# Layer norms of a decoder layer: mean and variance merged on VectorE, power and one pass per batch on GpSimd, and a new order of all engines

## The chip, the cores and the metric

The kernel runs on one core of a Trainium2 chip. A core has five engines that matter here: TensorE (PE in the profile; PEld is its weight load), VectorE (DVE), ScalarE (ACT), GpSimd (POOL) and SyncE (SP), whose queue issues all DMAs of this kernel. The metric is the device time of one execution in microseconds; the times given for a kernel are the median of several executions.

## The reference

One decoder layer without an outer batch loop: 64 sequences of 128 tokens with 128 features, a context of 77 tokens for each, 16 heads of 8.

```python
def _layernorm(x, axis=-1, eps=1e-05):
    m = jnp.mean(x, axis=axis, keepdims=True)
    v = jnp.var(x, axis=axis, keepdims=True)
    return (x - m) / jnp.sqrt(v + eps)

x = x + _L0_attn_ref(_layernorm(x, axis=-1), Wq, Wk, Wv, Wo)          # causal, window of 64
x = x + _L0_xattn_ref(_layernorm(x, axis=-1), ctx, ctx, mask, ...)    # 77 context tokens, additive mask
x = x + _L0_ffn_ref(_layernorm(x, axis=-1), W_r, W_k, W_v, mu_r, mu_k)
# ffn: r = sigmoid(xr @ W_r); k = square(relu(xk @ W_k)); out = r * (k @ W_v)
```

Each of the three blocks begins with a layer norm over the 128 features of a token. These norms are what the change is about.

## The kernel before, in words

**Tiles.** The 64 sequences are taken in 16 quads of four (`QB = 4`). A tile of activations is 128 partitions (tokens) by 4 sequences by 128 features, so 128x512. A quad `q` passes through self-attention, cross-attention and the feed-forward part; attention works on pairs `p` of sequences. `score_max` holds scores for the maxima, `score_exp` the scores for the exponentials, and there is one of each in PSUM, so scores, maxima and exponentials alternate on TensorE, VectorE and ScalarE. Two PSUM tiles `proj[0]` and `proj[1]` take all projections and transposes in turn.

**Order.** Every engine has its own list of calls, written out by hand in three parts: `fill()`, `step(s)` for s from 7 to 14, and `drain()`. A step works on several quads at once: it begins quad s, attends to quad s-1, starts the cross-attention's projections of quad s-2, does the cross-attention of s-3 and s-4, and ends the feed-forward part of quads s-4 and s-5. One step takes about 40 us. Each engine runs its list strictly in order; semaphores, with `wait_ge` ahead of an instruction, tie the lists together. A wait holds all that stands behind it on its engine.

**The norms.** There are three per quad, 48 in all: n = 0 on the input `x_in` for the self-attention, n = 1 on `x1` for the cross-attention, n = 2 on `x2` for the feed-forward part. Each goes this way:

1. VectorE, `stats_of` (L1420 to L1428): four `bn_stats`, one per sequence, from 128x128 each to six numbers, which are count, mean and sum of squared deviations of the even columns and of the odd ones.
2. GpSimd, `moments_of` (L643 to L663): three small operations on 128x4 combine both halves (L648 to L650), then three more (L653 to L655), then one (L658) gives four times the variance plus four epsilon; `pow` with -0.5 gives half of the reciprocal root (L660), and one addition doubles it (L663). Each group waits for the one before.
3. GpSimd, `norm_of` (L665 to L674): one pass over 128x512 subtracts the mean (L669), a second multiplies by the reciprocal root (L672), both with a broadcast operand. The output is `xn[n]`.
4. TensorE turns `xn` (`turn_x`, `turn_xc`, `turn_xe`, all with the line of the helper, L2021), ScalarE copies it out of PSUM (`take_xnT`, `take_xcT`, `take_xeT`), and the projections follow.

VectorE's `stats_of` waits before it writes: `ln_moments[n] >= 7 * q` says that GpSimd has used the statistics of the quad before.

**Other work that the text below names.** VectorE: `max_self` (L1553, L1556) and `max_cross` (L1565, `cneg_max`) take the maxima of scores, `copy_low` (L1544, `k_low`) copies key rows in pairs of instructions, `rest_k`, `rest_q`, `rest_ck`, `rest_cq` (L1499, L1501) split projections into bfloat16 parts, `mid_max` and `mid_cross_max` (L1574, L1581, `cmax_mid`) do so for maxima, `spread_v` (L1525, `v_heads`) writes the values, `add_x1` and `add_x2` (L1608, L1617) add the residual, `mix_tokens` (L1626) mixes neighbouring tokens, `split_mask` (L1449 and on, `mask_f`) prepares the mask once at the start. GpSimd: `low_part` (L681) makes the last bfloat16 part, `add_bias` (L689), `step_tokens` (L697), `square_key` (L702), `add_y` (L706), and at the start the fills of `make_self_pads` (L616, `v_even`, `v_odd`) and `make_cross_pads`. SP: the stores of the parts to DRAM (`store_k`, `store_q`, `k_scr`, `q_scr`), their loads in another layout (`load_keys`, `load_queries`, and the cross ones), `load_x`, `load_ctx`, `load_shift`, `load_cross_shift`, `store_y`. ScalarE: exponentials (`exp_self` L964, `exp_cross` L976) and copies, `take_v_odd` (L949) among them. TensorE: `attend_rest`, `attend_cross` (products with the probabilities), `mix_key`, `mix_gate`, `mix_value` of the feed-forward part.

## Time and profile before

| | |
|---|---|
| median of 3 executions | 778.36 us (778.01 to 781.46) |
| the profiled execution, its own time | 780.04 us |
| its span in the profile | 778.2 us |
| mean granted clock of TensorE, share of full | 0.898 |
| busy: PE, PEld, DVE, ACT, POOL | 647.1, 487.2, 515.7, 415.5, 379.6 us |
| DMA | 106.79 MB, 54.9% of 16 engines |
| a step in the middle of the run | about 40 us |

The profile is of one execution. The busy time of an engine is the sum of its instructions; register, branch and DMA-issuing instructions are not in it. The span is what the profile covers, and the execution's own time lies 1.8 us over it. "Idle before" in a row is the time in which an engine had nothing running ahead of that instruction, with what released it. The chain that ended last is followed back from the last instruction, at each step to what released it.

### The profile page before, as it was taken

The numbers are of one execution on the slowest core, as the hardware profiler recorded it, in microseconds if no ns is written. First come the engines' busy times: TensorE is split into PE (matmuls) and PEld (weight loads), VectorE is DVE, ScalarE is ACT, GpSimd is POOL, SyncE is SP. The second block draws the span as 40 slices with busy tenths as digits, with TensorE's granted clock in tenths as the row PEclk, the third lists the DMA queues.
The fourth block names the chain that finished last, engine by engine and source line by source line (L and its number), as shares of the span: only waits on it lengthen the run. The fifth ranks groups of instructions, "written<-read, shape, count | busy, mean of one in ns | idle before, by whom it ended". The sixth has DMA issues, their size and how long they took to land.

```text
span 778.2 us, 32657 instructions
## 1 busy us (share of the span) xinstructions
PE 647.1 (83%) x13935; PEld 487.2 (63%) x13935; DVE 515.7 (66%) x906; ACT 415.5 (53%) x634; POOL 379.6 (49%) x681
## 2 busy tenths in 40 slices
PE   2368778988988899999999999899899987997663
PEld 2247566766666676767677767677776765674442
DVE  8773556777666687777777777767677764754431
ACT  1122525665555666666666666566565663754430
POOL 7732323365444646473746464645365641634413
PEclk9555878999899999999999999999899996998875
DMA  2936585585664857475666666756567663333200
GB/s 69 174 121 88 151 163 159 133 176 141 167 161 104 209 126 195 105 222 114 186 150 169 161 176 149 189 134 174 141 164 169 165 155 53 103 93 101 51 15 13
DMA packets 162102, 106.79 MB, mean 137 GB/s; under 512 B 40531, under 2 KB 149414, under 8 KB 161958
## 3 DMA queue, kind: packets, MB, share of 16 engines
q1 hardware_dynamic: 161958, 104.70, 54.9%
q8 instruction: 111, 1.82, 1.1%
q14 instruction: 33, 0.27, 0.1%
HBM read 53.48 MB, written 50.14 MB: 133 GB/s over the span
## 4 chain that ended last, share of the span: by engine, by line
PE 56%; DVE 14%; POOL 11%; issue 9%; ACT 7%; DMA 2%; POOLq 0%; SPq 0%; DVEq 0%; ACTq 0%
PE sums L2253 5%; PE proj L2177 4%; PE proj L2021 4%; PE score_max L2091 4%; PE sums L2141 3%; PE score_exp L2235 3%; PE score_exp L2122 3%; PE sums L2153 2%; PE proj L2262 2%; PE proj L2201 2%; PE score_max L2220 2%; PE proj L2045 2%; PE proj L2081 2%; PE proj L2051 2%; DVE cneg_max L1565 2%
## 5 line engine op out<-in xcount | busy, mean ns | idle before, releaser
L976 ACT ACTIVATE cprobs<-score_exp 77x1024 f32<-77x1024 f32 x128 | 130.1, 1017 | 58.7 <-PE score_exp L2235 57.3
L1565 DVE TENSOR_REDUCE cneg_max<-score_max 128x8 f32<-128x616 f32 x128 | 102.0, 797 | 42.1 <-PE score_max L2220 40.1
L964 ACT ACTIVATE probs<-score_exp 128x1024 f32<-128x1024 f32 x96 | 97.7, 1018 | 56.8 <-PE score_exp L2122 35.8
L1553 DVE TENSOR_REDUCE neg_max<-score_max 128x8 f32<-128x1024 f32 x64 | 78.1, 1220 | 24.8 <-PE score_max L2091 24.4
L2253 PE MATMUL sums<-cprobs,cv_heads 128*32 128x128 f32 x2048 | 83.3, 294 | 3.5 <-ACT cprobs L976 3.2
L648 POOL TENSOR_TENSOR moments<-stats 128x4 f32<-128x4 f32 x48 | 11.6, 241 | 123.8 <-DVE stats L1428 123.7
L2235 PE MATMUL score_exp<-cq_stack,ck_stack 53*128 53x128 bf16 x1024 | 53.9, 227 | 16.6 <-ACT cprobs L976 15.3
L2021 PE MATMUL proj<-ident,xn 128*128 128x128 f32 x192 | 34.8, 311 | 37.2 <-POOL xn L672 35.6
L2253 PEld LDWEIGHTS sums<-cprobs,cv_heads 128*32 128x32 f32 x2048 | 53.5, 115 | 17.6 <-issue 6.8
L681 POOL TENSOR_TENSOR k_parts<-k_rest,k_parts 128x512 bf16<-128x512 f32 x16 | 18.6, 1162 | 90.7 <-ACT k_parts L879 90.7
L2235 PEld LDWEIGHTS score_exp<-cq_stack,ck_stack 53*128 53x128 bf16 x1024 | 31.2, 98 | 39.5 <-ACT cprobs L976 29.4
L672 POOL TENSOR_TENSOR xn<-xn,rstd 128x512 f32<-128x512 f32 x48 | 50.3, 1047 | 6.9
L660 POOL TENSOR_TENSOR root<-var_eps,neg_half 128x4 f32<-128x4 f32 x48 | 50.0, 1041 | 3.8
L2091 PE MATMUL score_max<-k_stack,q_stack 112*64 112x128 bf16 x1024 | 45.2, 236 | 7.6 <-DVE neg_max L1553 4.2
L1544 DVE COPY k_low<-k_stack 48x1024 bf16<-48x1024 bf16 x64 | 48.5, 798 | 3.1 <-DMA k_stack<-k_scr 2.2
L2021 PEld LDWEIGHTS proj<-ident,xn 128*128 128x128 f32 x192 | 23.7, 156 | 42.4 <-issue 40.5
L2122 PEld LDWEIGHTS score_exp<-q_stack,k_stack 114*128 114x128 bf16 x1024 | 40.2, 102 | 14.0 <-issue 9.5
L2220 PEld LDWEIGHTS score_max<-ck_stack,cq_stack 51*128 51x128 bf16 x1024 | 27.1, 99 | 34.9 <-DVE cneg_max L1565 21.0
L2220 PE MATMUL score_max<-ck_stack,cq_stack 51*128 51x77 bf16 x1024 | 41.8, 204 | 8.0 <-DVE cneg_max L1565 7.2
L2141 PE MATMUL sums<-probs,v_heads 128*32 128x64 f32 x2048 | 45.5, 234 | 2.3 <-ACT probs L964 1.7
L1556 DVE TENSOR_REDUCE neg_max<-score_max 128x16 f32<-128x1024 f32 x32 | 39.0, 1218 | 11.5 <-PE score_max L2104 11.4
L2091 PEld LDWEIGHTS score_max<-k_stack,q_stack 112*64 112x64 bf16 x1024 | 34.1, 119 | 18.1 <-DVE neg_max L1553 7.0
(162 smaller groups left out, 1472.9 us busy)
## 6 DMA issues: line engine op xcount, KB each, us to landing
k_stack<-k_scr SPq DMA_DIRECT2D x32, 384.0 KB, 5.0
q_stack<-q_scr SPq DMA_DIRECT2D x32, 384.0 KB, 5.2
cq_stack<-cq_scr SPq DMA_DIRECT2D x64, 192.0 KB, 3.5
ck_stack<-ck_scr SPq DMA_DIRECT2D x64, 125.1 KB
k_scr<-k_parts SPq DMA_DIRECT2D x16, 384.0 KB
q_scr<-q_parts SPq DMA_DIRECT2D x16, 384.0 KB, 3.4
cq_scr<-cq_parts SPq DMA_DIRECT2D x16, 384.0 KB
x_in<-in_x_dram SPq DMA_DIRECT2D x16, 256.0 KB, 4.1
```

Source lines behind the costliest of these rows:

```text
L672: nc.gpsimd.tensor_tensor(xn[n][:, :, :], xn[n][:, :, :], rstd[n][:, :].unsqueeze(2).to_broadcast([P, QB, D]), ALU.mult)\
L964: nc.scalar.activation(probs[:, k, :], score_exp[:, :], ACT.Exp).then_inc(exp_done, 1)
L976: nc.scalar.activation(cprobs[0:TC, n % CSLOTS, :], score_exp[0:TC, :], ACT.Exp).then_inc(cexp_done, 1)
L1553: nc.vector.tensor_reduce(neg_max[p][:, :, k, 1], score_max[:, :].rearrange("p (g k) -> p g k", g=G), AX_X, ALU.max, negate=True).then_inc ...
L1565: nc.vector.tensor_reduce(cneg_max[p][:, :, :, a, b], score_max[:, :].rearrange("p (j c) -> p j c", j=2)[:, :, 0:4 * TC] .rearrange("p j ( ...
L2021: last = nc.tensor.transpose(dst[:, rows * b:rows * b + rows], src[0:rows, b, :], ident[0:rows, 0:rows])
L2091: last = nc.tensor.matmul(score_max[HALF * a:HALF * a + HALF, T * g:T * g + T], q_stack[0:ROW1, p, a, g, b, HALF:T], k_stack[0:ROW1, p, a, ...
L2122: last = nc.tensor.matmul(score_exp[:, c:c + HALF], k_stack[0:ROWS_SELF, p, a, g, b, :], q_stack[0:ROWS_SELF, p, a, g, b, HALF:T], start=T ...
L2141: last = nc.tensor.matmul(sums[0][32 * i:32 * i + 32, b, a, HALF:T], v_heads[:, a, PB * p + b, g, :], probs[:, 2 * b, c:c + HALF], start=( ...
L2220: last = nc.tensor.matmul(score_max[:, c:c + TC], cq_stack[r:r + SHIFT_CROSS, p, i, a, b, :], ck_stack[r:r + SHIFT_CROSS, p, i, a, TC * b: ...
L2235: last = nc.tensor.matmul(score_exp[:, c:c + T], ck_stack[r:r + ROWS_CROSS, p, i, a, TC * b:TC * b + P], cq_stack[r:r + ROWS_CROSS, p, i, ...
L2253: last = nc.tensor.matmul(sums[1][32 * i:32 * i + 32, b, a, :], cv_heads[:, a, PB * p + b, g, :], cprobs[:, n % CSLOTS, c:c + T], start=(j ...
```

## The change

VectorE gets the merging of the statistics: after the four `bn_stats` it does four `bn_aggr`, one per sequence, each from six numbers to mean and variance, and one addition of epsilon to the four variances. Before the first `bn_aggr` it waits for the previous norm's `xn` of the same kind (`ln_out[n]`), since that pass reads `moments[n]`. `moments_of` is gone from GpSimd. `norm_of` waits for the variances, does the `pow`, waits for it, and then does one `tensor_scalar` for each of the four sequences, which subtracts the mean and multiplies by the reciprocal root, both given as one value per partition. The lists of all engines are in a new order: most of `fill()` and `drain()` have swaps of neighbours, and `step()` has a few.

```diff
-        moments = [sb(f"moments{n}", [P, 6, QB]) for n in range(3)]
+        moments = [sb(f"moments{n}", [P, QB, 2]) for n in range(3)]
         var_eps = [sb(f"var_eps{n}", [P, QB]) for n in range(3)]
-        root = [sb(f"root{n}", [P, QB]) for n in range(3)]
...
-        ln_root = [sem(f"ln_root{n}") for n in range(3)]
-        ln_centred = [sem(f"ln_centred{n}") for n in range(3)]
+        ln_var = [sem(f"ln_var{n}") for n in range(3)]
...
-            def moments_of(n, q):
-                pool.wait_ge(ln_stats[n], QB * q + QB)
...
             def norm_of(n, src, q, turned):
                 if later(q):
                     pool.wait_ge(turned, q)
-                mean = moments[n][:, 3, :].unsqueeze(2).to_broadcast([P, QB, D])
-                nc.gpsimd.tensor_tensor(xn[n][:, :, :], src[:, :, :], mean, ALU.subtract).then_inc(ln_centred[n], 1)
+                pool.wait_ge(ln_var[n], q + 1)
+                nc.gpsimd.tensor_tensor(rstd[n][:, :], var_eps[n][:, :], neg_half[:, :], ALU.pow).then_inc(ln_rstd[n], 1)
                 pool.wait_ge(ln_rstd[n], q + 1)
-                pool.wait_ge(ln_centred[n], q + 1)
-                nc.gpsimd.tensor_tensor(xn[n][:, :, :], xn[n][:, :, :],
-                                        rstd[n][:, :].unsqueeze(2).to_broadcast([P, QB, D]), ALU.mult)\
-                    .then_inc(ln_out[n], 1)
+                for b in range(QB):
+                    nc.gpsimd.tensor_scalar(xn[n][:, b, :], src[:, b, :], moments[n][:, b, 0:1], rstd[n][:, b:b + 1],
+                                            ALU.subtract, ALU.mult).then_inc(ln_out[n], 1)
...
                 if later(q):
-                    dve.wait_ge(ln_moments[n], 7 * q)
+                    dve.wait_ge(ln_moments[n], QB * q)
                 for b in range(QB):
                     nc.vector.bn_stats(stats[n][:, b, :], src[:, b, :]).then_inc(ln_stats[n], 1)
+                if later(q):
+                    dve.wait_ge(ln_out[n], QB * q)
+                for b in range(QB):
+                    dve.wait_ge(ln_stats[n], QB * q + b + 1)
+                    nc.vector.bn_aggr(moments[n][:, b, :], stats[n][:, b, :]).then_inc(ln_moments[n], 1)
+                dve.wait_ge(ln_moments[n], QB * q + QB)
+                nc.vector.tensor_scalar(var_eps[n][:, :], moments[n][:, :, 1], EPS, None, ALU.add).then_inc(ln_var[n], 1)
```

Waits of others on `ln_out`, `xn` among them, count four per quad in place of one. The moves in `step()`, engine by engine (SP, GpSimd, ScalarE, VectorE, TensorE):

```diff
-                load_x(q0)
                 load_cross_shift(q4, 1)
+                load_x(q0)
...
-                load_cross_queries(q3, 1)
                 load_cross_keys(q3, 1)
+                load_cross_queries(q3, 1)
...
                 norm_of(0, x_in[q0 % XSLOTS], q0, xnT_made)
-                add_y(q5)
                 low_part(k_parts, 0, k_rest, 1, k_left, k_mid, k_lo, k_stored, 48, q0)
                 low_part(q_parts, 2, q_rest, 1, q_left, q_mid, q_lo, q_stored, 48, q0)
-                moments_of(1, q2)
+                add_y(q5)
                 norm_of(1, x1[q2 % XSLOTS], q2, xcT_made)
...
-                take_v_odd(q1)
                 exp_cross(q4, 1, 1)
                 exp_cross(q4, 1, 2)
                 take_attT(q2, proj[(s + 1) % 2])
                 take_xnT(q0, proj[s % 2])
                 exp_cross(q4, 1, 3)
+                take_v_odd(q1)
...
+                take_cross_sums(q4, 1)
                 mid_q(q0)
-                take_cross_sums(q4, 1)
...
-                mid_max(q1, 1, proj[s % 2])
                 max_cross(q3, 1, 1)
+                mid_max(q1, 1, proj[s % 2])
...
-                attend_cross(q4, 1, 0, 0)
                 pe.wait_ge(v_ready, 3 * q1 + 2)
                 turn_sums(q2, 1, proj[s % 2])
                 pe.wait_ge(cexp_done, 8 * q4 + 6)
                 cross_scores(q4, 1, 1, 0)
+                attend_cross(q4, 1, 0, 0)
...
+                attend_cross(q3, 0, 1, 0)
                 pe.wait_ge(max_mid_ready, 2 * q1 + 2)
                 turn_xe(q4, proj[s % 2])
-                attend_cross(q3, 0, 1, 0)
...
+                pe.wait_ge(exp_done, 6 * q1 + 5)
+                scores_upper(q1, 1, 1)
                 pe.wait_ge(relu_ready, q4 + 1)
                 mix_gate(q4, proj[(s + 1) % 2])
-                pe.wait_ge(exp_done, 6 * q1 + 5)
-                scores_upper(q1, 1, 1)
```

At the start VectorE's list has these moves: `make_low_rows(0)` now stands ahead of the second `stats_of`, `split_mask` behind `order_biases`, and the fills for the second pair and the values of quad 0 change places; TensorE turns quad 1 and projects its keys before the first scores.

## Rows read from the trace of the kernel before

**Rows 1.** Page, first part, busy share of each engine
```profile
PE 647.1 (83%) x13935; PEld 487.2 (63%) x13935; DVE 515.7 (66%) x906; ACT 415.5 (53%) x634; POOL 379.6 (49%) x681
```

**Rows 2.** Page, fourth part, chain that ended last, by engine
```profile
PE 56%; DVE 14%; POOL 11%; issue 9%; ACT 7%; DMA 2%; POOLq 0%; SPq 0%; DVEq 0%; ACTq 0%
```

**Rows 3.** Windows; busy us of PE, PEld, DVE, ACT, POOL (instructions), clock, DMA
```profile
84.00:281.30 197.30, 170.89 (x3916) 128.51 (x3915) 129.42 (x236) 109.14 (x167) 92.55 (x175) 0.91 0.66 158
281.30:568.00 286.70, 263.57 (x6093) 201.64 (x6093) 215.07 (x379) 180.10 (x274) 156.99 (x288) 0.97 0.63 161
363.20:403.30 40.10, 36.90 (x871) 28.18 (x871) 30.87 (x55) 25.79 (x40) 22.47 (x42) 1.00 0.65 164
...
300.00:304.00 4.00, 2.72 (x128) 2.07 (x116) 3.87 (x6) 2.60 (x4) 3.55 (x5) 1.00 0.79 168
...
544.00:548.00 4.00, 2.13 (x96) 1.56 (x85) 3.55 (x5) 0.60 (x1) 2.58 (x4) 0.98 0.83 171
548.00:552.00 4.00, 3.55 (x52) 2.68 (x52) 1.08 (x2) 3.04 (x5) 1.94 (x2) 0.50 0.24 91
```

**Rows 4.** Waits of TensorE, until 300 us and from 300 to 600 us
```profile
PE proj L2021 <- POOL xn L672: 28.1, 7, 12.0
...
PE score_exp L2235 <- ACT cprobs L976: 9.8, 15, 0.9
```

**Rows 5.** Timeline of TensorE, its three longest waits for `xn`
```profile
12.02 1.09 PE L2021 MATMUL proj<-ident,xn 128*128 128x128 f32 x4 [12.02 <-POOL xn L672]
32.91 1.09 PE L2021 MATMUL proj<-ident,xn 128*128 128x128 f32 x4 [10.54 <-POOL xn L672]
...
763.38 1.09 PE L2021 MATMUL proj<-ident,xn 128*128 128x128 f32 x4 [7.06 <-POOL xn L672]
```

**Rows 6.** Timeline of all engines, the norm of `x_in` in a step
```profile
357.64 0.86 DVE L1428 BATCH_NORM_STATS2 stats<-x_in 128x6 f32<-128x128 f32 x4
...
358.58 0.20 POOL L648 TENSOR_TENSOR moments<-stats 128x4 f32<-128x4 f32 x1 [4.64 <-DVE stats L1428]
...
359.94 0.69 DVE L1525 COPY v_heads<-proj 128x512 f32<-128x512 f32 x1 [1.12 <-PE sums L2153]
...
362.64 1.04 POOL L672 TENSOR_TENSOR xn<-xn,rstd 128x512 f32<-128x512 f32 x1
...
363.82 0.63 PE L2021 MATMUL proj<-ident,xn 128*128 128x128 f32 x4
```

**Rows 7.** Groups of GpSimd by line: a pass and the power
```profile
L672 POOL TENSOR_TENSOR xn<-xn,rstd 128x512 f32<-128x512 f32 x48 | 50.3, 1047 | 6.9
L660 POOL TENSOR_TENSOR root<-var_eps,neg_half 128x4 f32<-128x4 f32 x48 | 50.0, 1041 | 3.8
```

**Rows 8.** Groups of VectorE by line and shape
```profile
L1428 DVE BATCH_NORM_STATS2 stats<-x 128x6 f32<-128x128 f32 x128 | 27.8, 279 | 0.6
...
L1478 DVE COPY bias_cols<-sums 128x3 f32<-128x3 f32 x1 | 0.1, 145 | 0.0
...
L1372 DVE MEMSET neg_half<- 128x4 f32 x1 | 0.1, 62 | 0.8 <-PEq L3370 0.8
```

**Rows 9.** Timeline of VectorE, idle time behind the other two norms' statistics
```profile
370.87 0.28 DVE L1581 TENSOR_TENSOR cmax_mid<-proj,cmax_hi 32x128 bf16<-32x128 f32 x1 [0.93 <-ACT cmax_hi L957]
...
381.39 0.75 DVE L1501 SCALAR_TENSOR_TENSOR cq_rest<-proj,bias_cols,cq_parts 128x512 f32<-128x512 f32 x1 [0.82 <-ACT cq_parts L875]
```

**Rows 10.** Timelines of VectorE and GpSimd; line L1544, ns min/median/max
```profile
10.90 4.66 DVE L1449 TENSOR_SCALAR mask_f<-mask_in 16x308 f32<-16x308 int32 x1
...
14.45 0.95 POOL L616 MEMSET v_odd<- 128x1024 f32 x1
...
363.97 1.56 DVE L1544 COPY k_low<-k_stack 48x1024 bf16<-48x1024 bf16 x2
...
383.31 2.02 DVE L1544 COPY k_low<-k_stack 48x1024 bf16<-48x1024 bf16 x2
...
L1544 DVE COPY k_low<-k_stack x64: 418/487/3815, 31.4 to 666.8; 48x1024 bf16<-48x1024 bf16 x64
```

953 lines of the change are left out of this document (457 added, 496 removed).

## The prediction

> **What bounds the kernel now.** The busy shares come first [rows 1]: TensorE leads with 83%, VectorE has 66%, GpSimd 49%. The chain that ended last says the same with one more name in it: 56% TensorE, but also 14% VectorE and 11% GpSimd, some 86 us of 778 [rows 2]. Averages over stages with different limits can mislead, so the windows come next [rows 3]. In the undisturbed step (363.2 to 403.3) TensorE is busy 36.9 of 40.1 us at full clock, VectorE 30.9, GpSimd 22.5. TensorE is the bound there and only 3.2 us a step can be won. Over the seven steps from 281.3 to 568 it is idle 23.1 us (286.7 less 263.6), and a step takes 41.0 us.
>
> The waits of TensorE tell what the norms cost it [rows 4]. Up to 300 us it waits 28.1 us in 7 waits for `xn`, the output of a norm; between 300 and 600 that wait is absent and the largest is 9.8 us for ScalarE's exponentials. Three single waits carry most of the total [rows 5]: 12.02 us at the start, 10.54 us before the second quad's turn, 7.06 us in the tail. What is left of the first 300 us is 28.1 - 12.0 - 10.5 = 5.5 us in five waits.
>
> **The chain of one norm.** In a step [rows 6] the statistics run from 357.64 to 358.50, GpSimd starts at 358.58, `xn` ends at 363.68, and TensorE turns it at 363.82. From statistics to `xn` it is 5.2 us: 2 x 1.04 the two passes over 512 columns, 1.04 the power, and the remaining 2.1 the seven small operations and the doubling, 0.2 us each, with their gaps [rows 6, 7].
>
> **VectorE's part.** It gets four aggregations of six numbers, a wait for the last, and one 4-column addition, 48 times. No such operation is in the trace. From below stands the 62 ns fill of 128x4 [rows 8], from above a statistics instruction, four of them in 0.86 us and 0.28 us for one alone [rows 6, 8]. I take a little less than the 145 ns of the 128x3 copy, the nearest in size [rows 8], as neighbours overlap: 5 x 0.12, and 0.1 us estimated for the wait, about the gap at GpSimd's hand-over [rows 6]. That is 0.7 us a norm; bounds 5 x 0.06 + 0.1 = 0.4 and 5 x 0.28 = 1.4. A step has three norms: 2.1 us, 30.9 to 33.0 of 40.
>
> What hides it: behind the three statistics of a step VectorE sits idle within one or two instructions: 1.12 us before `v_heads` [rows 6], 0.93 before `cmax_mid` and 0.82 before `cq_rest` [rows 9]. Each holds 0.7. I cost the addition at nothing in the step. If the cover is gone, every 0.1 us over it is 0.3 us a step. The third is the tight one: the maximum right behind the statistics of `x2` frees the score bank for the next maxima.
>
> **GpSimd's part.** Seven small operations and the doubling go, and 2 x 1.04 us of passes become four passes of 128 columns. From below a 4-column operation lasts 0.2 us [rows 6]; from above that plus a quarter of 1.04 is 0.46. I take 0.33, in the middle, 1.3 us in all (0.8 to 1.8). The chain is then 0.7 + 0.1 + 1.04 + 0.1 + 1.3 = 3.2 us, 2.0 us shorter (by the bounds 0.7 to 2.8). GpSimd's load falls from 22.5 by 3 x (8 x 0.2 + 2.1 - 1.3) to about 15 us a step.
>
> **A lock between the two engines.** `mask_f`, 16x308, takes 4.66 us and ends at 15.56, just after GpSimd's fill of `v_odd` ends at 15.40; `k_low` has a median of 0.49 us, so a pair takes about 1.0, but in the step one pair takes 1.56, beside `add_y`, and the other 2.02, beside the passes of the `x2` norm [rows 10]. So these copies wait for a running GpSimd instruction. The norm of `x2` will be done about 2 us earlier, before its pair begins, and `add_y` is moved away from the other: up to 0.6 + 1.0 us a step.
> The Trainium skill, "SBUF — State Buffer", section "Who interferes with whom", speaks against the change here: copy, cast and tensor_scalar may take VectorE's two-port mode, and then wait for a whole GpSimd instruction; the new addition of epsilon is a tensor_scalar. The trace agrees for `mask_f`. By that rule the sum would gain up to one GpSimd instruction, 1.04 us, at each norm.
>
> **The sum, by stage.**
> Start: the first norm is on the path, 2.0 us of 12.02. But VectorE's second `stats_of` now waits for the first `xn` before it aggregates, and the ordering of the biases, the mask and `rest_k` queue behind it. Behind that the chain goes through DMAs of `k_scr` and `q_scr`, which only move. The 10.54 us wait shrinks, but the first keys are awaited too. Taken: -2.0 (0 to -3).
> Build-up, 84 to 281: five waits of 5.5 us together, each shorter than the 2.0 us won; what is late next (projections' outputs, exponentials) takes a third back. Taken: -3.5 (0 to -5.5).
> Steps: TensorE is not seen waiting for `xn`; the turn of `xn` follows it by 0.14 us [rows 6], and of the 1.6 us of collisions [rows 10] the second stands ahead of `cneg_max`, for which TensorE waits; part of it pays for the 0.7 us of VectorE ahead. I take 0.5 us a step from both, eight steps: -4.0 (+4 to -9).
> Tail: the last norm is alone on the path, -2.0, and I add an estimated -0.4 for the norms of the two quads before, which wait beside other work: -2.4 (-0.7 to -3.2).
> Moved steps, at 0 each: on SP's queue `load_x` goes behind the two DMAs of a cross shift, whose wait now holds it too, but its tile is read only by the last statistics of the step; the swap of cross keys and queries exchanges like with like, and the stores behind keep their place. On GpSimd's queue `add_y` goes behind the k and q parts, which wait for ScalarE; `add_x2` waits for it, and comes later in the step. TensorE turns `xe` and does `mix_gate` behind one group of products each; the mixing behind it waits for a maximum on VectorE anyway. ScalarE's copy of `v_odd` goes behind three exponentials and is read by `attend_rest`, a third of a step on. If a cover fails, the moved work is late by what it was moved past, at most one exponential (1 us) a step; I allow -1 to +3 us for all of them.
> Sum: -2.0 - 3.5 - 4.0 - 2.4 = -11.9. The profiled execution took 780.04 us (span 778.2); it lies 1.7 above the median 778.36. So 768.1 for such an execution, and 766.5 as the median.
>
> **The rivals.**
> Hidden anyway. TensorE is the bound and no wait for `xn` stands in the steps [rows 3, 4]. Only the tail and 1 us at the start remain: 775.4. Against it: five waits in the build-up.
> More than forecast. A step in the middle takes 41.0 us on average and 40.1 undisturbed, and in 548 to 552 TensorE ran at a granted clock of 0.50, the lower of its two levels (1.2 GHz), right behind 4 us in which it was busy 2.1 [rows 3]. If the shorter chain removes the idle time ahead of such stretches, 0.9 us in each of seven steps come back: 766.5 - 6 = 760.5. For it: a clock mean of 0.97 and 0.91 in two stages. Against: the idle time there is mostly VectorE's and ScalarE's.
> VectorE becomes the bound: slower. Place: the third statistics of a step, ahead of the maximum and the `k_low` copies. It decides when a norm adds more than its gaps hold, 0.96 us on average; at 1.2 the gains are eaten (0.24 x 3 x 13 steps = 9.4, and the gain of the steps with it). At the upper bound of 1.4 it costs 0.44 x 3 x 13 = 17 us: 783.5. For it: VectorE is busy 3.9 of 4 us in 300 to 304, and TensorE only 2.7 [rows 3]. Against: small operations are cheap there.
> The lock at every norm: slower. If the addition of epsilon waits as `mask_f` and `k_low` do [rows 10], its cost hangs on GpSimd. Busy 15 of 40 us with instructions of 1.04 at most, GpSimd is met in four cases of ten and for half an instruction, 0.2 us a norm, which the gaps hold. A whole instruction each time would make 0.7 + 1.04 = 1.74, 0.78 over the gaps, 30 us in all: 796.5.
> The change does not do what it says: four passes at 0.46 us with two scalars each cost 1.8 of the 2.2 they replace. Then a norm wins 1.5 of the 2.0 us, a quarter of the sum goes, and the time is 769.5; it falls in the forecast's own range.
>
> **How the numbers follow.** A measurement of this kernel can tell about 0.5%, 3.9 us: 774.5 and 782.3 are the bounds. Chances: forecast (762 to 774.5) 0.50; more than forecast 0.18; hidden anyway 0.20; slower by VectorE 0.09; by the lock 0.03. Faster 0.68, same 0.20, slower 0.12. The range, 755 to 782, takes in the larger gain, the hidden case, and leaves most of the slow case out.
>
> **What would show it.** Right: aggregations near 0.12 us apart; four passes of 0.3 to 0.35; `xn` about 3.2 us behind the statistics; the tail wait 5 us in place of 7.06; the five early waits gone; `k_low` pairs near 1.0 us; steps of 40 us. Wrong: VectorE busy over 34 us a step, waits of TensorE for `cneg_max` grown, the addition of epsilon at 0.5 us or more (the lock), or a start no earlier because VectorE waits for `xn`. A new idle stretch from the reordering alone would show as a wait for something that no norm feeds.

## The result, and the profile after

The changed kernel takes 802.63 us (median of 4 executions, 795.49 to 805.95). The kernel before, run beside it on the same chip, takes 779.91 us. The ratio is 1.0268, with an interval of 1.0179 to 1.0356: slower by about 21 us, where a gain of 12 was forecast, and outside the range. The profiled execution took 801.91 us with a span of 800.1. The ratios here and below leave out every execution over 1.5% above the fastest of its own kernel, and so they can differ from the quotient of the two medians.

The first and fourth parts of the page:

```profile
PE 642.9 (80%) x13935; PEld 485.1 (61%) x13935; DVE 520.0 (65%) x1146; ACT 418.0 (52%) x634; POOL 364.2 (46%) x393
...
PE 49%; DVE 15%; POOL 14%; issue 9%; ACT 6%; DMA 5%; SPq 1%; POOLq 0%; DVEq 0%; ACTq 0%
```

TensorE's busy time fell by 4 us against [rows 1] while the span grew by 22, so the loss is idle time. The working said that GpSimd falls from 22.5 to about 15 us a step, which over 16 quads is 120 us; in the whole run it fell by 15, from 379.6 to 364.2. On the chain GpSimd went from 11 to 14% and TensorE from 56 to 49% [rows 2].

The groups of GpSimd and VectorE by line and shape (busy us, mean ns of one, idle before):

```profile
L648 POOL TENSOR_SCALAR xn<-x,moments,rstd 128x128 f32<-128x128 f32 x128 | 104.5, 829 | 3.3
...
L648 POOL TENSOR_SCALAR xn<-x_in,moments,rstd 128x128 f32<-128x128 f32 x64 | 53.6, 848 | 1.7
...
L645 POOL TENSOR_TENSOR rstd<-var_eps,neg_half 128x4 f32<-128x4 f32 x48 | 52.1, 1085 | 130.6 <-DVE var_eps L1383 130.5
...
L1499 DVE COPY k_low<-k_stack 48x1024 bf16<-48x1024 bf16 x64 | 28.6, 487 | 3.9 <-DMA k_stack<-k_scr 2.9
...
L1383 DVE TENSOR_SCALAR var_eps<-moments 128x4 f32<-128x4 f32 x48 | 19.9, 416 | 1.6
...
L1381 DVE BATCH_NORM_AGGREGATE moments<-stats 128x2 f32<-128x6 f32 x192 | 17.4, 152 | 2.3 <-POOL xn L648 2.3
```

A pass over 128 columns takes 0.83 us on average, not 0.33: the four of a norm take 3.14 us in the timeline below, more than the two wide passes of 1.04 [rows 7] that they replace. The 192 passes cost 158 us, where the 96 wide ones cost 100. The small operations that went away pay for that and for VectorE's new part, and little more, and so the norm hardly got shorter. This is the norm of `x_in` in a step, the answer to [rows 6], in the timeline of all engines:

```profile
367.78 0.86 DVE L1376 BATCH_NORM_STATS2 stats<-x_in 128x6 f32<-128x128 f32 x4
...
368.57 0.36 DVE L1381 BATCH_NORM_AGGREGATE moments<-stats 128x2 f32<-128x6 f32 x4
...
368.96 0.17 DVE L1383 TENSOR_SCALAR var_eps<-moments 128x4 f32<-128x4 f32 x1
...
369.28 1.03 POOL L645 TENSOR_TENSOR rstd<-var_eps,neg_half 128x4 f32<-128x4 f32 x1 [5.18 <-DVE var_eps L1383]
...
370.41 3.14 POOL L648 TENSOR_SCALAR xn<-x_in,moments,rstd 128x128 f32<-128x128 f32 x4
...
373.98 0.60 PE L1983 MATMUL proj<-ident,xn 128*128 128x128 f32 x4
```

From the end of the statistics (368.64) to the end of `xn` (373.55) it is 4.9 us, against 5.2 before and 3.2 forecast. VectorE's share of it is 0.5 us at this norm, at the low end of its term; one of the other two norms of a step is dearer, as the part on the lock says.

TensorE's waits until 300 us (total, times, longest) answer to [rows 4]:

```profile
PE proj L1983 <- POOL xn L648: 31.3, 8, 11.6
PE score_max L2053 <- DVE neg_max L1508: 6.1, 5, 2.2
PE score_max L2066 <- DVE neg_max L1508: 3.4, 5, 1.3
```

The waits for `xn` did not shrink, they grew from 28.1 to 31.3 us. Where the time went is read best from when VectorE begins the statistics of `x_in` of each quad (a table made from the timelines, us; the third kernel is norms_only of the next section, the last one is the kernel before with a test of single operations behind its whole work):

| quad | 3 | 4 | 5 | 6 | 7 | 14 | 15 | end |
|---|---|---|---|---|---|---|---|---|
| before | 107.2 | 146.6 | 187.2 | 231.4 | 275.7 | 562.3 | 601.1 | 778.2 |
| after | 107.0 | 139.7 | 190.9 | 241.2 | 287.6 | 576.6 | 615.8 | 800.1 |
| changed norms, old order | 107.2 | 144.7 | 189.5 | 229.9 | 275.5 | 557.1 | 600.3 | 777.2 |
| before, in probe | 102.1 | 142.2 | 183.1 | 223.3 | 264.7 | 550.1 | 592.5 | |

After is 7 us ahead of before at quad 4 and 12 behind at quad 7. The seven steps add 2.4 us, the tail 7. Each line is one execution, and such a clock scatters: the last line runs the same instructions up to its tail as the first, and is 11 us ahead of it at quad 7. Five profiles with the changed norms and the old build-up until there begin quad 6 between 226.4 and 231.9 us (norms_only, old_fill, new_step_only, new_step_old_pool, fill_c). So a difference of 4 or 5 us between two such lines says little. The changed kernel's 241.2 at quad 6 is beyond it, and the other two profiles with the whole new build-up and these norms agree, with 239.6 and 241.9. The windows say the same (columns as in [rows 3]); after, then before:

```profile
130.00:180.00 50.00, 41.57 (x1022) 30.72 (x1019) 32.45 (x73) 28.24 (x42) 18.77 (x21) 0.94 0.67 147
180.00:230.00 50.00, 41.04 (x947) 31.06 (x944) 35.36 (x73) 29.10 (x45) 23.20 (x25) 0.97 0.60 140
230.00:290.00 60.00, 50.77 (x1163) 38.79 (x1165) 39.45 (x90) 31.04 (x48) 24.64 (x26) 0.94 0.63 136
```

```profile
130.00:180.00 50.00, 45.05 (x1121) 33.40 (x1118) 36.07 (x62) 31.32 (x47) 22.49 (x41) 0.95 0.69 163
180.00:230.00 50.00, 45.16 (x973) 34.04 (x973) 32.38 (x60) 29.10 (x46) 22.38 (x41) 0.93 0.59 146
230.00:290.00 60.00, 54.10 (x1207) 40.20 (x1205) 42.75 (x82) 35.13 (x56) 31.01 (x56) 0.97 0.62 141
```

TensorE is busy 133.4 of these 160 us, 144.3 before. The mean granted clock is nearly the same in both (0.94, 0.97, 0.94 and 0.95, 0.93, 0.97), so the clock is not what took the time.

### The profile page after: what moved, and what is told of

Read it like the earlier page. It is cut to its first block, busy times and chain, and to the rows that moved or that the text cites. A ratio compares the mean times of both kernels' runs of the same rounds, so it can differ in the third digit from the quotient of the medians.

```text
span 800.1 us, 32606 instructions
## 1 busy us (share of the span) xinstructions
PE 642.9 (80%) x13935; PEld 485.1 (61%) x13935; DVE 520.0 (65%) x1146; ACT 418.0 (52%) x634; POOL 364.2 (46%) x393
## 4 chain that ended last, share of the span: by engine, by line
PE 49%; DVE 15%; POOL 14%; issue 9%; ACT 6%; DMA 5%; SPq 1%; POOLq 0%; DVEq 0%; ACTq 0%
POOL xn L648 8%; PE sums L2215 5%; PE proj L2139 4%; PE score_exp L2197 3%; PE proj L1983 3%; PE sums L2103 3%; PE sums L2115 3%; POOL rstd L645 3%; DMA q_stack<-q_scr 3%; PE proj L2224 3%; PE score_max L2053 3%; PE score_exp L2084 2%; PE score_max L2182 2%; PE proj L2007 2%; PE proj L2163 2%
## 5 line engine op out<-in xcount | busy, mean ns | idle before, releaser
L1520 DVE TENSOR_REDUCE cneg_max<-score_max 128x8 f32<-128x616 f32 x128 | 102.1, 798 | 43.1 <-PE score_max L2182 42.4
L645 POOL TENSOR_TENSOR rstd<-var_eps,neg_half 128x4 f32<-128x4 f32 x48 | 52.1, 1085 | 130.6 <-DVE var_eps L1383 130.5
L648 POOL TENSOR_SCALAR xn<-x,moments,rstd 128x128 f32<-128x128 f32 x128 | 104.5, 829 | 3.3
L1508 DVE TENSOR_REDUCE neg_max<-score_max 128x8 f32<-128x1024 f32 x64 | 78.0, 1218 | 29.0 <-PE score_max L2053 28.6
L648 POOL TENSOR_SCALAR xn<-x_in,moments,rstd 128x128 f32<-128x128 f32 x64 | 53.6, 848 | 1.7
L2084 PE MATMUL score_exp<-q_stack,k_stack 114*128 114x64 bf16 x1024 | 43.5, 198 | 3.0 <-ACT probs L912 2.5
```

Of the source, the lines that this page charges most:

```text
L645: nc.gpsimd.tensor_tensor(rstd[n][:, :], var_eps[n][:, :], neg_half[:, :], ALU.pow).then_inc(ln_rstd[n], 1)
L648: nc.gpsimd.tensor_scalar(xn[n][:, b, :], src[:, b, :], moments[n][:, b, 0:1], rstd[n][:, b:b + 1], ALU.subtract, ALU.mult).then_inc(ln_ou ...
L1508: nc.vector.tensor_reduce(neg_max[p][:, :, k, 1], score_max[:, :].rearrange("p (g k) -> p g k", g=G), AX_X, ALU.max, negate=True).then_inc ...
L1520: nc.vector.tensor_reduce(cneg_max[p][:, :, :, a, b], score_max[:, :].rearrange("p (j c) -> p j c", j=2)[:, :, 0:4 * TC] .rearrange("p j ( ...
L2084: last = nc.tensor.matmul(score_exp[:, c:c + HALF], k_stack[0:ROWS_SELF, p, a, g, b, :], q_stack[0:ROWS_SELF, p, a, g, b, HALF:T], start=T ...
```

## The experiments

Executions of one kernel scatter by 5 to 20 us (eleven of the kernel before on one chip lie between 763.2 and 784.9), and so ratios are given with their intervals, and traces are used to place a loss. "Old order" is the order of the kernel before in `fill()`, `step()` and `drain()`.

**The change cut in two.** norms_only has the changed norms in the old order; the other has the old norms in the new order, with `moments_of` directly ahead of each `norm_of`, where the kernel before has it at all but two places.

```diff
 # norms_only
-                mean = moments[n][:, 3, :].unsqueeze(2).to_broadcast([P, QB, D])
+                for b in range(QB):
+                    nc.gpsimd.tensor_scalar(xn[n][:, b, :], src[:, b, :], moments[n][:, b, 0:1], rstd[n][:, b:b + 1],
...
 # order_only, TensorE and GpSimd
-                turn_att(2, proj[1])
+                turn_x(4, proj[1])
+                pe.wait_ge(att_ready, 6)
+                turn_att(2, proj[0])
...
-                add_y(q5)
...
+                add_y(q5)
+                moments_of(1, q2)
                 norm_of(1, x1[q2 % XSLOTS], q2, xcT_made)
```

> The changed norms (merge on VectorE, power, four narrow passes on GpSimd) in the order of before. Theory A, the narrow passes: each lasts 0.83 us instead of the 0.33 that I took, so the loss of some 22 us is theirs and stays here: 795 to 802 us. Theory B, the new order: a norm takes 4.9 us from its statistics to its output in the changed kernel's step against 5.2 before, so in the old order nothing is lost: 774 to 781 us. Theory C, VectorE's added 0.9 us a norm: loss spread evenly over the steps, 785 to 795 us.

Measured: 781.88 us, ratio 1.0080 (1.0024 to 1.0135). That is 0.9 us above the range of theory B and far below those of A and C.

> The norms of before in the new order, each moments_of right ahead of its norm_of. Theory A: the order is harmless, 775 to 782 us. Theory B: the loss is here, 795 us or more, most of it between 140 and 290 us and in the tail.

Measured: 810.91 us, ratio 1.0384 (1.0292 to 1.0475). Theory B holds. The norms alone cost a little instead of gaining; the larger part is the order.

**The narrow passes taken back**: VectorE still merges, GpSimd has two wide passes again. Once in the old order, once in the changed kernel.

```diff
-                for b in range(QB):
-                    nc.gpsimd.tensor_scalar(xn[n][:, b, :], src[:, b, :], moments[n][:, b, 0:1], rstd[n][:, b:b + 1],
-                                            ALU.subtract, ALU.mult).then_inc(ln_out[n], 1)
+                nc.gpsimd.tensor_tensor(xn[n][:, :, :], src[:, :, :], moments[n][:, :, 0:1].to_broadcast([P, QB, D]),
+                                        ALU.subtract).then_inc(ln_centred[n], 1)
+                pool.wait_ge(ln_centred[n], q + 1)
+                nc.gpsimd.tensor_tensor(xn[n][:, :, :], xn[n][:, :, :],
+                                        rstd[n][:, :].unsqueeze(2).to_broadcast([P, QB, D]), ALU.mult)\
+                    .then_inc(ln_out[n], QB)
```

> Merge on VectorE, but the two passes of 128x512 of before (1.04 us each), in the order of before: GpSimd's chain is 1.04 + 0.1 + 2.2 us, about 1.0 us shorter a norm than in the changed kernel. Theory A: 770 to 776 us, the gain that I had forecast. Theory C, VectorE's added time is what costs: 780 to 790 us. Theory B says only that it is not above the norms_only kernel.

Measured: 777.79 us, ratio 1.0005 (0.9964 to 1.0046): between the ranges of A and C, so neither the forecast's gain nor a loss.

> The changed kernel with the two wide passes in place of the four narrow ones. Theory A: the loss goes, 765 to 778 us. Theory B: the order keeps most of it, 790 us or more. If both act, in between, and the difference to the changed kernel is the price of the narrow passes in this order.

Measured: 791.54 us, ratio 1.0170 (1.0106 to 1.0235). Against norms_only (1.0080) and the changed kernel (1.0268) the narrow passes thus cost 0.8 and 1.0%, 6 to 8 us; the two intervals overlap in each case, the sign is the same in both, and by the medians of norms_only and merge_wide_old_order, measured side by side, it is 4.1 us. The new order, in turn, costs 1.65% with these norms (13.8 us between the medians, 791.54 less 777.79), 1.9% with the changed ones (some 15 us) and 3.8% with the old ones (some 30 us, 23 to 37 by the interval). The first two can't be told apart. The old norms, which load GpSimd most, pay most for the new order; that the length of a norm's chain is the reason is not shown.

merge_wide_old_order is the fair test of the forecast's main idea, since there the chain of a norm is really shorter (the wait in the tail falls from 7.06 to 5.82 us, so by 1.2) and GpSimd is busy 307.7 us in place of 379.6. Its waits of TensorE in the whole run, then those of the kernel before:

```profile
PE proj L1987 <- POOL xn L651: 25.2, 4, 10.0
...
PE proj L2228 <- DVE mixed L1585: 8.5, 11, 2.9
...
PE score_max L2057 <- DMA q_stack<-q_scr: 7.2, 6, 3.4
```

```profile
PE proj L2021 <- POOL xn L672: 35.6, 10, 12.0
...
PE proj L2262 <- DVE mixed L1626: 7.1, 12, 2.9
...
PE score_max L2091 <- DMA q_stack<-q_scr: 1.4, 2, 1.0
```

The waits for `xn` fall by 10.4 us, as the forecast wanted, and all five early ones are gone: none stands between 29 and 706 us. The time does not fall, because other waits take the place. The scores of the next pair now wait for their queries from DRAM, 7.2 us in place of 1.4, and those for `mixed` grow a little. The shorter norm is hidden behind what comes next.

VectorE's new part takes some of it as well. In every step it stands between the statistics of `x1` and the rest of the queries, `q_rest`. The kernel before, then merge_wide_old_order:

```profile
286.57 0.86 DVE L1428 BATCH_NORM_STATS2 stats<-x 128x6 f32<-128x128 f32 x4
287.35 0.67 DVE L1499 TENSOR_TENSOR q_rest<-proj,q_parts 128x512 f32<-128x512 f32 x1
```

```profile
285.89 0.86 DVE L1380 BATCH_NORM_STATS2 stats<-x 128x6 f32<-128x128 f32 x4
...
287.06 1.09 DVE L1387 TENSOR_SCALAR var_eps<-moments 128x4 f32<-128x4 f32 x1
288.07 0.68 DVE L1458 TENSOR_TENSOR q_rest<-proj,q_parts 128x512 f32<-128x512 f32 x1
```

`q_rest` begins 2.18 us after the statistics in place of 0.78, in each of the eight steps. No run has the shorter norm without this, so how much of the missing gain it ate is open.

**What a pass costs.** Behind the whole work of the kernel before, GpSimd runs single operations four times each, alone; then VectorE and ScalarE run the same.

```diff
+            for r in range(4):
+                nc.gpsimd.tensor_scalar(x_step[:, r, :], src[:, r, :], mm, rr, ALU.subtract, ALU.mult).then_inc(probe_done, 1)
...
+                nc.gpsimd.tensor_scalar(xn[1][:, r, :], src[:, r, :], 0.5, 2.0, ALU.subtract, ALU.mult).then_inc(probe_done, 1)
...
+                nc.gpsimd.tensor_tensor(attT[:, r, :], src[:, r, :], src[:, 0, :], ALU.mult).then_inc(probe_done, 1)
```

> The kernel of before, and behind its last addition on GpSimd rows of single operations into tiles no longer used: tensor_scalar on 128x128 with two values per partition, with two constants, with one value per partition; tensor_tensor on 128x128; tensor_scalar with two values on 128x64, 128x4 and 128x512, and with two constants on 128x512; then the same two-value operation on VectorE, and a scaled and biased activation on ScalarE. Theory P1, a fixed price of fetching the two values: 128x4 at 0.6 us and 128x512 at 1.5 us. Theory P2, a slow element loop: 0.8 us at 128, 0.5 at 64, 0.2 at 4, 2.5 or more at 512, and constants as slow. The runtime of the whole says nothing here.

The groups by line (two values per partition at 128, 4 and 512 columns; two constants; one value; two tensors; VectorE):

```profile
L859 POOL TENSOR_SCALAR x_step<-xn,moments,rstd 128x128 f32<-128x128 f32 x4 | 3.2, 796 | 0.1
...
L861 POOL TENSOR_SCALAR xn<-xn 128x128 f32<-128x128 f32 x4 | 2.5, 641 | 0.0
...
L863 POOL TENSOR_SCALAR xn<-xn,rstd 128x128 f32<-128x128 f32 x4 | 2.4, 603 | 0.0
...
L871 POOL TENSOR_SCALAR craw<-xn,moments,rstd 128x512 f32<-128x512 f32 x1 | 2.1, 2089 | 0.0
...
L865 POOL TENSOR_TENSOR attT<-xn 128x128 f32<-128x128 f32 x4 | 1.6, 442 | 0.0
...
L869 POOL TENSOR_SCALAR k_relu<-xn,moments,rstd 128x4 f32<-128x4 f32 x4 | 1.5, 388 | 0.0
...
L2026 DVE TENSOR_SCALAR mixed<-xn,moments,rstd 128x128 f32<-128x128 f32 x4 | 1.1, 342 | 22.7 <-POOL x L873 22.7
```

Between 4 and 512 columns it is (2089 - 388) / 508 = 3.35 ns a column on 0.37 us that do not depend on the width. A product of two tensors of 128 columns takes 442 ns. So the pass with two values per partition has both a start of 0.37 us, paid four times, and about twice the price per column of the broadcast `tensor_tensor` (an estimate from 1047 less 200, over 512 columns: 1.7 ns). One wide instruction would not have helped, it costs 2.09 us, what the two wide passes took. Neither a mere start cost (theory P1, which had 1.5 us for 512 columns) nor a mere column cost (P2, which had 0.2 us for 4) explains it. Two constants in place of the two values make it 641 ns, one value 603. VectorE does the same in 0.34 us.
The Trainium skill, "GPSIMD Engine Reference", section "Elementwise — side-by-side cycle accounting", gives at best 1.8 cycles per element with one input, 768 ns for 512 elements, and 2.6 cycles with two inputs. The rows do not agree for this form: 512 columns take 2089 ns, and with 128 columns the one-input form (796 ns) costs more than the two-input one (442 ns).

**The new order cut into its three parts.** All with the changed norms.

```diff
 # old_fill: fill() of all engines as before; old_drain: drain() as before; new_step_only: fill() and drain() as before
-                turn_x(4, proj[1])
-                pe.wait_ge(att_ready, 6)
-                turn_att(2, proj[0])
+                turn_att(2, proj[1])
...
```

> The changed kernel with the old order in fill() alone; step() and drain() in the new order. The quads' own clock (start of the statistics of x_in) puts the changed kernel 12 us behind at quad 7, and quads 14 and 15 with the tail add another 7.6. Theory B1, the order of the fill: 788 to 792 us. Theory B2, the order of the drain: the fill is harmless, 798 to 803 us.

> The changed kernel with the old order in drain() alone. Theory B1: 796 to 803 us, the loss of the fill stays. Theory B2: 786 to 792 us. If both parts act, each of the two kernels gets back its own share and the shares add up to the 21 us between the changed kernel and norms_only.

> The changed norms with the new order in step() alone, the old one in fill() and drain(). Theory B (either): the eight steps are not where it is lost, 779 to 785 us. Rival: the step's own moves (add_y ahead of the norm of x1) hold that norm back by 1.3 us a step, which makes 788 us or more.

Measured: old_fill 789.31 us, 1.0192 (1.0127 to 1.0256); old_drain 797.37, 1.0318 (1.0248 to 1.0387); new_step_only 785.45, 1.0141 (1.0078 to 1.0205). The first two fall in the ranges of theory B1; new_step_only lies between its two, half a microsecond above the one without a loss. The new build-up is worth 1.8% between the last two. By the medians the old drain gives nothing back, and old_fill less new_step_only would give 0.5% for the new one, within the intervals.

The profiles say something that the medians do not. From the statistics of quad 14 to the end, the fourteen with the old drain take 215.6 to 226.3 us. With the new drain wide_new_order, old_fill, order_only and after_repaired take 228.9 to 231.3, the changed kernel 223.5. In wide_new_order quad 14 begins only 4.7 us later than in merge_wide_old_order (561.2 and 556.5), and the end comes 17.3 us later. So the new drain probably has a share of the loss too, with wide passes the larger one in these two profiles; no pair of medians shows it.

Next, the new build-up alone, and each third of it alone. The lists of all engines were cut where both orders have done the same calls, at about 140 and 240 us.

```diff
 # fill_b, TensorE (one of its places); new_fill_only has all, fill_a those until 140 us, fill_c those behind 240 us
-                turn_att(2, proj[1])
+                turn_x(4, proj[1])
+                pe.wait_ge(att_ready, 6)
+                turn_att(2, proj[0])
...
-                project_k(5, proj[1])
                 pe.wait_ge(cmax_taken, 19)
                 cross_max(2, 0, 1, 1)
-                pe.wait_ge(x1_ready, 4)
-                project_q(5, proj[0])
+                pe.wait_ge(xnT_ready, 6)
+                project_k(5, proj[1])
...
```

> Changed norms, new order in fill() of all engines, old order in step() and drain(). Theory M (the new build-up order is the larger half of the loss from the order): ratio 1.018 to 1.030, against 1.008 for the changed norms in the old order. Rival N (the loss needs the new step as well, the build-up alone costs little): 1.008 to 1.013.

> As new_fill_only, but only the first of three parts of the new build-up is taken (until about 140 us: the start, the quads 0 to 3, the cross-attention of quad 0); the rest is in the old order. Theory M: the first part costs nothing, since in the changed kernel the statistics of quad 4 begin 7 us earlier than before and not later: 1.008, within 0.5%. Rival N (work done early at the start makes a hole later): 1.015 or more.

> Only the middle part of the new build-up (about 140 to 240 us), where the norm of quad 4 is taken ahead of the cross-attention and the self-attention of quads 2 and 3, and its turn and projection of keys stand ahead of the turn and output projection of quad 2; the rest is in the old order. Theory M: this part carries the loss, since the statistics of x_in of quads 4 to 6 stand 51 and 50 us apart in the changed kernel and 41 and 44 before: 1.016 to 1.028, nearly that of new_fill_only. Rival N: no part alone costs it, 1.008 to 1.012 here.

> Only the last part of the new build-up (about 240 to 290 us); the rest is in the old order. Theory M: nearly nothing, 1.008 to 1.012. Rival N: a third of what new_fill_only costs over the changed norms in the old order.

Measured: new_fill_only 794.52 us, 1.0234 (1.0197 to 1.0270); fill_a 781.66, 1.0098 (1.0055 to 1.0140); fill_b 789.88, 1.0170 (1.0129 to 1.0211); fill_c 787.12 beside 776.68 of the kernel before, with executions from 773.28 to 788.50 and no ratio that holds, so it stays inconclusive. The middle third carries the larger part of the build-up's loss with the changed norms, as theory M had it; new_fill_only costs more than it alone, with intervals that overlap.

**Inside the middle third**: fill_b1 takes only the early quad 4, fill_b2 all the rest.

```diff
 # fill_b1
-                turn_att(2, proj[1])
+                turn_x(4, proj[1])
+                pe.wait_ge(att_ready, 6)
+                turn_att(2, proj[0])
...
 # fill_b2, ScalarE
+                mid_k(5)
+                high_q(5, proj[0])
                 take_cross_max(2, 0, proj[1])
-                mid_q(5)
                 take_cross_sums(1, 1)
-                exp_self(4, 0, 1)
+                take_v_odd(4)
                 take_ctxT(3, proj[1])
+                mid_q(5)
```

> Of fill_b only its head: VectorE's statistics of quad 4 one third earlier, TensorE's turn of quad 4 and its projection of keys ahead of the turn of quad 2 and its output projection, ScalarE's copies in the same exchange, GpSimd's add_bias(0) behind the norm of quad 4. Theory E (the early quad 4 is what costs: it delays x1 of quad 2 and with it the cross-attention that all later quads stand behind): 1.014 to 1.022, and the statistics of quad 5 begin 3 us later than with the changed norms in the old order (189.47), those of quad 6 6 us or more later (229.89). Rival S (the swaps behind it do it): 1.008 to 1.012, quad 6 within 2 us.

> Of fill_b all but its head, so quad 4 in its old place and the later swaps of the build-up until about 240 us in the new order. Theory E: 1.008 to 1.012, quad 6 at 230 to 233. Rival S: 1.014 to 1.022, quad 6 at 235 or later.

Measured beside a kernel before of 777.06 us: fill_b1 782.98, fill_b2 790.53. Their ratios, 1.0186 (1.0102 to 1.0270) and 1.0257 (1.0160 to 1.0355), rest on three executions of the kernel before, so the two are compared with each other: 7.5 us apart. The statistics of quad 6 begin at 229.75 and 237.74 (229.89 with the changed norms in the old order). Theory E, which was mine, wanted the larger loss in fill_b1; it falls by the comparison of the two and by quad 6, though fill_b1's ratio by itself lies in its range. The swaps behind the early quad 4 cost more than it does. fill_b, which has both, takes 789.88 us and begins quad 6 at 234.36.

TensorE's timeline of fill_b2 has four waits of 5.5 us together, where norms_only has none over 0.74:

```profile
214.98 0.63 PE L1983 MATMUL proj<-ident,xn 128*128 128x128 f32 x4 [1.81 <-POOL xn L648]
...
218.09 0.64 PE L2215 MATMUL sums<-cprobs,cv_heads 128*32 128x128 f32 x16 [1.12 <-ACT cprobs L924]
...
223.84 0.63 PE L1983 MATMUL proj<-ident,xn 128*128 128x128 f32 x4 [1.30 <-POOL xn L648]
...
229.25 0.64 PE L2053 MATMUL score_max<-k_stack,q_stack 112*64 112x128 bf16 x16 [1.29 <-DVE neg_max L1508]
```

Next came the place of the two turns alone (fill_b3), the swaps ahead of it alone (fill_b4), and the changed kernel without it (after_repaired).

```diff
 # fill_b3; after_repaired is its reverse in the changed kernel
-                project_co(1, proj[1])
+                turn_xc(3, proj[1])
...
-                turn_xc(3, proj[0])
+                project_co(1, proj[0])
...
+                turn_xe(1, proj[1])
...
-                turn_xe(1, proj[1])
 # fill_b4
-                project_q(5, proj[0])
...
                 attend_cross(1, 1, 0, 1)
+                pe.wait_ge(x1_ready, 4)
+                project_q(5, proj[0])
```

> Changed norms in the old order, with one place of the new order only: TensorE turns xn of x1 (quad 3) ahead of the output projection of the cross-attention of quad 1, and xn of x2 (quad 1) ahead of the scores it followed; the copies and maxima of that stretch go with it. Theory E2 (this place carries the cost: TensorE reaches both turns before GpSimd's xn is there, 1.8 and 1.3 us, and maxima and exponentials behind them are late too, 1.3 and 1.1 us): four waits of TensorE of 5.5 us together appear near 210 to 230, the statistics of quad 6 begin 6 us or more later than 229.9, median near 788 to 791 us. Rival S2 (the loss is spread over all swaps): under 2 us, quad 6 before 233, median 781 to 785.

> Changed norms in the old order, with the swaps between the turn of quad 4 and that place (about 150 to 200 us) in the new order. Theory E2: nothing, median 780 to 784 us, no wait for xn over 1 us between 205 and 230, quad 6 at 230 to 233. Rival S2: 784 to 788, quad 6 at 234 or later.

> The changed kernel with that one place back in the old order, all else new. Theory E2: the changed kernel's 7 us of it come back, 802.6 to 794 to 797, ratio 1.018 to 1.023 against 1.0268. Rival S2: within 2 us of the changed kernel, ratio 1.025 or more.

Measured: fill_b3 782.63 us, 1.0111 (1.0060 to 1.0162); fill_b4 781.47, 1.0106 (1.0057 to 1.0154); after_repaired 795.67, 1.0278 (1.0234 to 1.0321). Neither alone is distinguishable from the changed norms in the old order (1.0080). Quad 6 begins at 231.9 and 234.1, against 237.7 in fill_b2, but the first lies within the scatter of the old order and the second little beyond it, and at quad 7 fill_b4 (282.6) is no earlier than fill_b2 (281.3). fill_b2 also has further swaps that neither of the two has, just behind that place and on SP's queue. Theory E2, one place alone, falls with fill_b3. S2, a loss spread over all swaps, is not excluded: its ranges hold for fill_b3 and for the ratio of after_repaired, and in fill_b4 for quad 6 but not for the time. The repaired kernel begins quad 6 at 233.8 in place of 241.2 and ends its profile at 793.1 in place of 800.1, as E2 had it, but its ratio shows no gain; it stays open how much of that place comes back in the median.

GpSimd's timelines tell how the two places act on each other. The norm of `x1` of quad 3 stands behind the q part of quad 5 in its list. norms_only:

```profile
203.91 1.15 POOL L656 TENSOR_TENSOR q_parts<-q_rest,q_parts 128x512 bf16<-128x512 f32 x1 [0.77 <-ACT q_parts L827]
205.02 1.03 POOL L645 TENSOR_TENSOR rstd<-var_eps,neg_half 128x4 f32<-128x4 f32 x1
206.15 3.13 POOL L648 TENSOR_SCALAR xn<-x,moments,rstd 128x128 f32<-128x128 f32 x4
```

The changed kernel:

```profile
210.18 1.17 POOL L656 TENSOR_TENSOR q_parts<-q_rest,q_parts 128x512 bf16<-128x512 f32 x1 [3.43 <-ACT q_parts L827]
211.30 1.03 POOL L645 TENSOR_TENSOR rstd<-var_eps,neg_half 128x4 f32<-128x4 f32 x1
212.43 3.14 POOL L648 TENSOR_SCALAR xn<-x,moments,rstd 128x128 f32<-128x128 f32 x4
```

The swaps (TensorE projects the queries of quad 5 later, ScalarE does `mid_k` ahead of `high_q` and `take_v_odd` ahead of `mid_q`) make the q part wait 3.4 us for ScalarE in place of 0.8: so in fill_b2, after_repaired, wide_new_order and the changed kernel, 3.5 in fill_b4, and 0.77 in norms_only and fill_b3. That holds the norm behind it. The other place asks for that norm's output earlier. The first wait shows this in every profile: it is 1.8 us where both are (fill_b, fill_b2, new_fill_only, old_drain, the changed kernel), 0.7 with the swaps alone (fill_b4, after_repaired), and absent with the place alone (fill_b3).

The maxima and exponentials behind it are late with it. All waits of TensorE from 205 to 235 us come to 7.3 us in fill_b2 and fill_b, 3.3 in fill_b3, 2.9 in fill_b4 and 1.4 in norms_only: here both together cost 5.9 us over norms_only, where each alone costs 1.9 and 1.5.

That this is what the order costs as a whole is not shown. With the shorter norms the same stretch waits 5.4 us in wide_new_order and 3.6 in merge_wide_old_order, so 1.8 us more, and the order costs nearly as much as with the changed norms (13.8 and some 15 us). There the larger part must come from elsewhere.

**The step.** GpSimd's list in the step as before (`add_y` ahead of the k and q parts), the rest of new_step_only kept.

```diff
                 norm_of(0, x_in[q0 % XSLOTS], q0, xnT_made)
+                add_y(q5)
...
-                add_y(q5)
                 norm_of(1, x1[q2 % XSLOTS], q2, xcT_made)
```

> Changed norms, old build-up and drain, new step, but GpSimd's list in the step as before: add_y stands ahead of the k and q parts again. Theory A (add_y right ahead of the norm of x1 holds that norm, which is what the step's 0.6% come from: 1.0141 with it moved, 1.008 without the new step): 1.007 to 1.011. Rival B (the step's cost is in the lists of the other engines): 1.012 to 1.016.

Measured: 781.22 us beside 777.06; on the same chip fill_b1, which has the old step, took 782.98. The ratio, 1.0158 (1.0070 to 1.0246), lies in the range of rival B and rests on the same three executions of the kernel before. The medians speak for theory A (781.22 over 777.06 is 1.0054); nothing is decided. The traces show the mechanism. GpSimd in a step of the changed kernel:

```profile
301.85 1.16 POOL L656 TENSOR_TENSOR q_parts<-q_rest,q_parts 128x512 bf16<-128x512 f32 x1 [1.44 <-ACT q_parts L827]
302.97 1.28 POOL L681 TENSOR_TENSOR y_gated<-y_gated,x 128x512 f32<-128x512 f32 x1
304.21 1.03 POOL L645 TENSOR_TENSOR rstd<-var_eps,neg_half 128x4 f32<-128x4 f32 x1
305.34 3.14 POOL L648 TENSOR_SCALAR xn<-x,moments,rstd 128x128 f32<-128x128 f32 x4
```

From the end of the q part (303.01) to the end of `xn` (308.48) it is 5.5 us, and TensorE waits 0.41 us for it at 308.62; this stretch stands in the chain that ended last. In the kernel before it is 290.70 to 295.75, 5.1 us, without a wait. TensorE's waits between 290 and 600 us in new_step_only have `xn` with 3.0 us in 8; in new_step_old_pool it is not among them. The price is small, about 0.4 us a step, and not enough for a verdict: old_fill has the whole new step and runs from quad 7 to 14 in 280.1 us, new_step_only in 285.9, norms_only in 281.6, the kernel before in 286.6. A step's stretch without any change of the order scatters as much. What the new step costs in the median is left open.

## Why the prediction was wrong, step by step

**VectorE's part: right in price, not in "at nothing in the step".** 0.7 us a norm forecast, 0.36 and 0.17 measured where nothing holds it, 0.5 in all; four aggregations are 0.09 us apart. At the norm of `x1` in each step the addition is held and takes 1.09, and `q_rest` right behind it begins 1.4 us later than in the kernel before. The forecast looked for cover in the gaps behind, and in the changed kernel seven of the eight held additions stand in the chain that ended last. VectorE did not become the bound: its busy time rose by 4 us, since 37 us of new instructions came but others got shorter, `k_low` by 20 us above all.

**GpSimd's part: the step that failed first.** The term "from above that plus a quarter of 1.04 is 0.46. I take 0.33" priced a `tensor_scalar` with two per-partition values by the `tensor_tensor` beside it. It is another program on this engine with 0.37 us of start and 3.35 ns a column: 0.80 us, beyond even the upper bound. A bound taken from another form of instruction was no bound. The chain became 4.9 us, not 3.2, and the "2.0 us shorter" became 0.3. The narrow passes cost 0.8 to 1.0% against wide ones. The rival "the change does not do what it says" named this and kept the wrong end of the range (0.46), so it ended at 769.5.

**The build-up: the reason itself failed.** "five waits of 5.5 us together, each shorter than the 2.0 us won" gave -3.5. merge_wide_old_order wins 1.2 us at a norm by itself, 1.8 behind the q part of a step (5.1 us before, 3.3 there), removes all five waits and takes 10.4 us off the waits for `xn`, and its ratio is 1.0005; the low end of the interval, 0.9964, is a gain of 2.8 us. The term "takes a third back" was too small: other waits took all of it back. "Hidden anyway" was the right rival for the norms, and with 0.20 it had too little. For the changed norms as they are even it was too kind: 1.0080.

**Moved steps at 0: the step with the largest error.** "I allow -1 to +3 us for all of them" met 13.8 us with the shortest norms and 1.9%, some 15 us, with the changed ones (ratios 1.0268 and 1.0080). The working weighed the few moves of `step()` one by one and gave the hundreds of moved lines in `fill()` and `drain()` no term of their own. With the changed norms the loss stands mostly in the build-up (new_fill_only, 1.0234 against 1.0080), more of it in the middle third than in the first. One mechanism there is seen, norms that queue on GpSimd behind a late q part while TensorE asks for them earlier, with some 6 us of waits. What makes up the rest stays open, in the build-up as in the drain. `add_y`, put down as moved behind parts "which wait for ScalarE", was seen; that it then stands directly ahead of the norm of `x1`, and all of it in that norm's chain, was not.

**The lock: half right.** `k_low` fell from 48.5 to 28.6 us of VectorE, so most collisions are gone, as forecast, and this too gave no time; the order did much of it (32.7 with the old norms in the new order, 38.0 with the new norms in the old). The addition of epsilon does meet the lock, once a step, beside the k part of the next quad: eight times about 1.09 us in place of 0.17, twice about 0.9 in the build-up, and once 3.1 at the start. That is 0.9 us a step ahead of `q_rest`, and not the 0.78 at every norm of the rival. The forecast named the sign, "the addition of epsilon at 0.5 us or more (the lock)", and it came for one norm of three. What it costs in time was not tested by itself.

**Steps and tail.** -4.0 and -2.4 were forecast; seven steps took 2.4 us more, the tail wait went from 7.06 to 6.8. A longer tail of 7 us is in the profile. The old drain does not bring it back in the median, though the profiles part by drain: from quad 14 to the end 215.6 to 226.3 us with the old one, 223.5 to 231.3 with the new. Which of its moves does it is open.

**What the profile was to show.** "four passes of 0.3 to 0.35", "`xn` about 3.2 us behind the statistics", "the five early waits gone": all wrong for the changed kernel. "A new idle stretch from the reordering alone would show as a wait for something that no norm feeds": the waits for `neg_max` and for the copies of values are of that kind, but the first of them stands at a norm.

## What to carry to other kernels

Price an instruction by a row of the same form on the same engine; where none is there, the range is open to both sides, and a neighbour with another operand pattern is no end of it. An order list is worth what it costs by itself: this one lost time with all three kinds of norms, 1.7, 1.9 and 3.8%, and so it has to be measured apart from the change that it comes with. When a change rewrites such a list, read each moved call for what queues behind it on its engine and for who asks for that output, and allow as much for the pairs of moves as for the moves. A wait that vanishes is worth only the distance to the next one, which a variant that removes the wait alone will show. Two executions of the same code can be 11 us apart in the middle of the run, so let several profiles speak before a few microseconds are placed.

## What the runs showed of the hardware

A VectorE instruction can be held through several GpSimd instructions in a row. At the start of the changed kernel the addition of epsilon, 0.17 us otherwise, takes 3.10 us and ends at 15.03, while GpSimd fills three tiles back to back until 15.01:

```profile
11.93 3.10 DVE L1383 TENSOR_SCALAR var_eps<-moments 128x4 f32<-128x4 f32 x1
```

```profile
11.43 1.80 POOL L614 MEMSET v_heads<- 128x2048 f32 x1
13.18 0.94 POOL L614 MEMSET v_even<- 128x1024 f32 x1
14.06 0.95 POOL L614 MEMSET v_odd<- 128x1024 f32 x1
```

The Trainium skill, "SBUF — State Buffer", section "Who interferes with whom", says that whoever of the two issues first gets the shared ports for its whole instruction and the other fully blocks, and counts `tensor_scalar` among the operations that can be hit. These rows agree and go further, since the addition got in at none of the two changes from one fill to the next. All seventeen profiles with this addition show the same 3.10 us there. In the step it is held as long as one two-tensor operation runs (1.09 us, beside `k_parts`, 1.16). It seems to go the other way too: `xn` takes 5.08 us in place of 3.14 at 26.45, while VectorE copies `k_stack` and `q_stack` (1.22 us each from 26.83 and 28.09).
